# Router columns in the latent product, interleaved first-stage work, expert results added by scatter, and output products placed in the attention drain

## The reference, cut to what matters

```python
xn = layernorm(x)
# layer 0, attention (16 heads, latent): q_latent 192 wide, kv_latent 64 wide, k_rope 64 wide
lat = xn @ [q_a_w, kv_a_w].T ; q_latent, kv_latent = layernorm with weight and bias
scores = (q_nope.k_nope + q_rope.k_rope) * scale ; attn = softmax(scores) @ v ; out @ o_w.T
# layer 0, feed-forward: 32 experts, 4 a token, at most 128 tokens an expert
x2 = w_norm * xn * rsqrt(mean(xn*xn) + 1e-6)
probs = softmax(x2 @ w_router) ; w_topk, sel = top_k(probs, 4)
y[e] = (silu(buf[e] @ w_gate[e]) * (buf[e] @ w_up[e])) @ w_down[e]
out[token] += w_topk * y[e][place]              # tokens past the 128th of an expert are dropped
shared = sigmoid(x2 @ w_shared_gate) * ((silu(x2 @ sw_gate) * (x2 @ sw_up)) @ sw_down)   # 704 wide
x = x + attention + (xn + out + shared)
# layer 1: block-sparse attention and a low-rank expert feed-forward (not touched)
```

## Time and profile before

| what | us |
|---|---|
| runs of the kernel before | 750.59, 755.54, 756.66 (median 755.54) |
| the profiled execution's own time | 748.44 |
| its span, first to last instruction | 746.6 |

### The profile page before, as it was taken

One profiled execution on the slowest core, in us unless ns is written; L12 is line 12 of the kernel. 1 busy time (PEld: TensorE's weight loads), 2 busy tenths in 40 slices (PEclk: granted clock), 3 DMA queues, 4 the chain that ended last, 5 costly groups with the idle time before them and its releaser, 6 DMA issues.

```text
span 746.6 us, 11749 instructions
## 1 busy us (share of the span) xinstructions
PE 710.5 (95%) x3912; PEld 536.0 (72%) x3912; DVE 470.8 (63%) x1336; ACT 357.9 (48%) x928; POOL 262.6 (35%) x252
## 2 busy tenths in 40 slices
PE   4998989899999999998999989999899999999998
PEld 3787868789888898887776656666566648666557
DVE  5798786777887778876885876777633502144311
ACT  2732047688878888788212577898421100011000
POOL 0486125565655655551004248990000250000000
PEclk9999999999999999999999988999999999999999
DMA  8801124534535344343700002000300000000000
GB/s 327 310 1 40 53 81 112 161 112 165 175 99 182 99 162 130 112 146 113 316 1 0 1 1 100 2 2 6 110 0 1 0 1 21 8 0 1 0 1 28
DMA packets 26923, 59.40 MB, mean 80 GB/s; under 512 B 3226, under 2 KB 12956, under 8 KB 26480
## 3 DMA queue, kind: packets, MB, share of 16 engines
q1 hardware_dynamic: 23792, 50.45, 20.1%
q0 software_dynamic: 3072, 8.20, 3.4%
HBM read 48.35 MB, written 10.49 MB: 79 GB/s over the span
## 4 chain that ended last, share of the span: by engine, by line
PE 53%; DVE 10%; ACT 5%; issue 3%; POOL 0%; DMA 0%; DVEq 0%; ACTq 0%; POOLq 0%
PE bank L1975 10%; PE bank L2021 7%; PE bank L1983 7%; PE bank L2033 4%; PE bank L1763 3%; PE bank L1698 3%; PE bank L1867 3%; PE bank L1929 3%; PE bank L1913 2%; PE bank L1783 2%; PE bank L1754 2%; PE bank L1705 2%; PE bank L1774 2%; PE bank L1940 2%; DVE sb L1410 2%
## 5 line engine op out<-in xcount | busy, mean ns | idle before, releaser
L1045 ACT ACTIVATE sb<-bank 128x512 f32<-128x512 f32 x28 | 16.7, 597 | 148.2 <-PE bank L1975 148.2
L909 ACT ACTIVATE sb<-bank,sb 128x256 f32<-128x256 f32 x128 | 59.5, 470 | 40.2 <-DVE sb L1324 38.0
L1763 PE MATMUL bank<-sb 128*128 128x256 f32 x256 | 65.7, 379 | 0.0
L1560 DVE TENSOR_TENSOR sb<-sb,bank 128x512 f32<-128x512 f32 x28 | 19.3, 688 | 73.6 <-ACT sb L1045 73.6
L1324 DVE TENSOR_REDUCE sb<-bank 128x2 f32<-128x512 f32 x64 | 44.1, 689 | 26.0 <-PE bank L1763 24.8
L1009 ACT ACTIVATE sb<-sb 128x128 f32<-128x128 f32 (+1 forms) x128 | 50.6, 444 | 15.7 <-DVE sb L1510 15.1
L916 ACT ACTIVATE sb<-sb 128x256 f32<-128x256 f32 x128 | 57.5, 503 | 0.0
L1975 PE MATMUL bank<-rounded,b_hi 128*128 128x512 f32 x112 | 55.1, 492 | 0.0
L1983 PE MATMUL bank<-sb 128*128 128x512 f32 x112 | 52.8, 594 | 1.2 <-issue 0.7
L735 POOL DMA_INDIRECT sb<-rows_x,sb x32 | 33.0, 1032 | 48.3 <-PE bank L1698 27.2
L1698 PE MATMUL bank<-sb 128*128 128x128 f32 (+1 forms) x384 | 48.8, 277 | 0.8 <-DVE sb L1260 0.8
(11 more groups left out here) (260 smaller groups left out, 1622.9 us busy)
## 6 DMA issues: line engine op xcount, KB each, us to landing
sb<-in_w_gate_up SPq DMA_DIRECT2D x32, 368.0 KB
sb<-in_w_down SPq DMA_DIRECT2D x32, 256.0 KB
sb<-in_w_pair SPq DMA_DIRECT2D x8, 704.0 KB
expert_out<-sb SPq DMA_DIRECT2D x1, 4096.0 KB, 22.2
sb<-expert_out SPq DMA_DIRECT2D x8, 512.0 KB, 7.6
sb<-in_w SPq DMA_DIRECT2D x1, 1792.0 KB, 13.0
sb<-in_b SPq DMA_DIRECT2D x1, 1792.0 KB, 7.6
sb<-in_sw_up SPq DMA_DIRECT2D x1, 1536.0 KB, 8.5
```

What stands on the lines that cost most here:

```text
L909: act.activation(probs[:, u % 4, q, :], bank[3 + u % 2][:, q * S:(q + 1) * S], ACT.Exp, scale=-1.0, bias=row_min[:, u % 4, q:q + 1], accum ...
L1763: mm = pe.matmul(bank[3 + u % 2][:, q * S:(q + 1) * S], qb[i][:, h, b * S + q * P:b * S + (q + 1) * P], keys[:, h, b * S:(b + 1) * S], sta ...
```

## The change

1. The router's 32 columns, the shared gate's one and a column with `w_norm` join `w_lat` (418 columns, 417 of them multiplied). POOL scales the 33 by `w_norm` in place once `w_lat` has landed; PE waits for that before the first latent tile. The router's product (L1620), `w_route` and `x2T` go. DVE scales the 33 columns of all tiles by `rrms` and takes maxima and differences in three operations.
2. The transposes of x2 stand after latent tiles 4 to 7, ACT evicts only the high part, DVE takes the low part from PSUM (`x2_low`), four pieces, the last behind the router's differences. Shared unit 1 waits for all four ahead of its first matmul.
3. The last column tile of the shared part holds 64 gate and 64 up columns, so units 10 and 11 have 6 matmuls instead of 12.
4. The eviction of the transposed latents: three copies go to ACT (`latents_copied`), the two differences stay on DVE. Tiles 2, 3 are turned after unit 11. The addition of xn goes from POOL to ACT: acc = acc * (1 + rstd) - mean * rstd. The router's exponentials come after the first two shared units on ACT.
5. `merge_qk`, `merge_vo` and the four projections of pair 0 stand between the down tiles 4 to 7, in banks of their own. The pair loop waits for six tiles; the eighth is waited for ahead of the first expert. DVE's work on pair 0 stands between the sums in the same way.
6. The zeros go. `rows_x2` rows hold 256 values and 32 probabilities, written by two DMAs; a gather brings both. DVE scales an expert's result by its probability during the eviction. `acc` is written to `expert_sums` after the eighth shared sum, and every store is an indirect DMA that adds to it, issued when the store before it has landed. After the last one SP loads the eight sums into `acc`. The weighted additions L1410 go.
7. CLOSE is experts 26 to 31.
8. Output products of tiles 0 to 3 are issued in the drain, one after each of the first four values, in banks 0, 1, 3, 4. Layer 1's first product waits for four sums instead of eight.

```diff
-CLOSE = (0, 1, 2, 26, 27, 28, 29, 30, 31)
+CLOSE = range(E0 - 6, E0)
+OUT_BANK = (0, 1, 3, 4, 0, 1, 0, 1)
+OUT_AFTER = (0, 0, 0, 0, 1, 2, 5, 6)
-FIRST_TURNS = {2 * NF - 3: (0, 1), 2 * NF - 2: (2, 3)}
+FIRST_TURNS = {2 * NF - 3: (0, 1), 2 * NF - 1: (2, 3)}
+DOWN_BANK, DOWN_AFTER = (0, 1, 2, 3, 0, 3, 1, 2), (0, 0, 0, 0, 1, 4, 2, 3)
...
 # SP
-            sp.wait_ge(zero_set, 1)
-            sp.dma_start(res.rearrange("(r p) d -> p r d", p=P), along(zeros, (1, NT * TOPK0))).then_inc(rows_out_done, 16)
             sp.wait_ge(x2_done, NT)
-            sp.dma_start(rows_x2.rearrange("(t p) d -> p t d", p=P), x2).then_inc(rows_out_done, 16)
+            sp.dma_start(rows_t[:, :, 0:D], x2).then_inc(rows_out_done, 16)
+            sp.wait_ge(rt_step, 5)
+            sp.dma_start(rows_t[:, :, D:D + E0], prob).then_inc(rows_out_done, 16)
...
             sp.wait_ge(rt_dest, 1)
+            sp.wait_ge(rows_out_done, 32)
             for i in range(2):
                 pair_weights(i, i)
+            sp.wait_ge(sh_add, NT)
+            sp.dma_start(sums_t, acc).then_inc(rows_out_done, 16)
...
 # POOL
+            pool.wait_ge(lat_in, 16)
+            pool.tensor_tensor(w_lat[:, :, LATW:LATX], w_lat[:, :, LATW:LATX],
+                               w_lat[:, :, LATX:LATX + 1].broadcast_to([P, KD, E0 + 1]), ALU.mult).then_inc(route_scaled, 1)
...
             def store(e, s):
                 pool.wait_ge(ex_y, e + 1)
+                if e:
+                    pool.wait_ge(y_stored[(e - 1) % SETS], 16 * ((e - 1) // SETS) + 16)
+                else:
+                    pool.wait_ge(rows_out_done, 48)
+                pool.indirect_dma_start(sums[:, :], bass.IndirectOffsetOnAxis(ap=source[:, e:e + 1], axis=0), ye[:, s, :], None,
+                                        bounds_check=TOK - 1, oob_is_err=False, compute_op=ALU.add).then_inc(y_stored[s], 16)
...
 # ACT
+            for u in range(2):
+                shared_hidden(u)
+            act.wait_ge(rt_sub, 3)
+            act.activation(expo, logit, ACT.Exp).then_inc(rt_exp, 1)
+            act.activation(gate_e, scored[:, :, E0], ACT.Exp, scale=-1.0).then_inc(rt_exp, 1)
+            for u in range(2, 2 * NF):
+                shared_hidden(u)
+                for i in FIRST_TURNS.get(u, ()):
+                    latents_copied(i)
+                if 0 <= u - 3 < NT:
...
+                    act.activation(acc[:, i, :], acc[:, i, :], ACT.Identity, scale=grown[:, i:i + 1], bias=shift[:, i:i + 1])\
+                        .then_inc(acc_done, 1)
...
 # DVE
             for i in range(NT):
                 dve.wait_ge(lat_out, i + 1)
...
+                if i:
+                    latent_mean(i - 1)
+                if i > HALF:
+                    x2_low(i - 1)
+            latent_mean(NT - 1)
...
+            dve.tensor_tensor(scored, lat[:, :, LATW:LATX], along(rrms, (2, E0 + 1)), ALU.mult).then_inc(rt_sub, 1)
+            dve.wait_ge(rt_sub, 1)
+            dve.tensor_reduce(route_max, scored[:, :, 0:E0], AX.X, ALU.max).then_inc(rt_sub, 1)
+            dve.wait_ge(rt_sub, 2)
+            dve.tensor_tensor(logit, scored[:, :, 0:E0], along(route_max, (2, E0)), ALU.subtract).then_inc(rt_sub, 1)
+            x2_low(NT - 1)
...
             for i in range(NT):
                 dve.wait_ge(gathered[i], 16)
-                for k in range(TOPK0):
-                    j = i * TOPK0 + k
-                    if k:
-                        dve.wait_ge(combined, j)
-                    dve.scalar_tensor_tensor(acc[:, i, :], picked[:, TILE_AT[i] * TOPK0 + k, :], weight4[:, j:j + 1], acc[:, i, :],
-                                             ALU.mult, ALU.add).then_inc(combined, 1)
                 dve.wait_ge(op_mm, i + 1)
...
 # PE: latents, then the down stage, then the drain
+                if i >= HALF:
+                    turn(i, x2, x2_done)
...
+                if i == HALF:
+                    pe.wait_ge(latT_out, 2 * NT)
+                    merge_qk(0, 0, 0, bank[4])
+                    merge_vo(0, 0, bank[5])
+                if i == HALF + 1:
+                    pe.wait_ge(rt_dest, 1)
+                    pe.wait_ge(at_eff, 1)
+                    project(0, 0, 0, bank[6])
+                    pe.wait_ge(at_eff, 2)
+                    project(0, 1, 0, bank[5])
...
+            pe.wait_ge(sh_add, NT - 2)
...
                 values(g - VALUE_LAG, (g - VALUE_LAG) % UNITS)
+                if g - G < HALF:
+                    attention_out(g - G)
...
-            pe.wait_ge(op_add, NT)
+            pe.wait_ge(op_add, HALF)
```

More of the change, by code:

```diff
@@ L206, in lay_out @@
     kva = f["L0_attn_kv_a_w"]
[L207 to L208 removed]
+    w_lat = np.concatenate([f["L0_attn_q_a_w"], kva[:KVL], kva[KVL:][ROPE_ORDER], swap(kva[KVL:])[ROPE_ORDER]]).T
+    out["w_lat"] = tiles(np.concatenate([w_lat, f["L0_ffn_w_router"], f["L0_ffn_w_shared_gate"],
+                                         f["L0_ffn_w_norm"].reshape(D, 1)], 1))
     wq = f["L0_attn_q_b_w"].reshape(PAIRS, 2, DN, QL).transpose(0, 2, 1, 3)
@@ L379, in program @@
         r2 = strip(region2)
-        lat = r2.take(NT, LATW)
-        w_lat = r2.take(KD, LATW)
-        w_route = r2.take(KD, P)
+        lat = r2.take(NT, LATX)
+        ids = r2.take_b(2, NT * TOPK0, E0)
+        w_lat = Strip(region2, NT * LATX, KD * (LATX + 1)).take(KD, LATX + 1)
         sw_up = r2.take(KD, 2 * NF * P)
@@ L388, in program @@
         onehot = r2.take(NT, TOPK0, E0)
-        place4, over = r2.take(NT * TOPK0), r2.take(NT * TOPK0)
-        slot_id, slot_empty, slot_q, slot_r, token_f, dest_f = (r2.take(E0) for _ in range(6))
+        place4 = r2.take(NT * TOPK0)
+        slot_id, slot_empty, token_f = (r2.take(E0) for _ in range(3))
         hot = Strip(region1, 2 * NT * D, NT * D).take_b(NT * TOPK0, CAP)
-        ids = Strip(region2, NT * LATW, KD * (LATW + P)).take_b(2, NT * TOPK0, E0)
         su_hi = su_hi[:, :].rearrange("p (k n) -> p k n", k=KD)
@@ L851, in turned_copy, with x2_high @@
                     .then_inc(turned_out, 1)
+            def x2_high(g):
+                act.wait_ge(turned, g + 1)
+                act.activation(r(x2T_hi[:, :, (g % 4) * 2 * P:(g % 4 + 1) * 2 * P]),
+                               bank[turn_bank(g)][:, :].rearrange("p (k n) -> p k n", k=KD), ACT.Copy).then_inc(turned_out, 1)
             for g in range(2):
@@ L856, in _ @@
                 act.wait_ge(lat_mm, i + 1)
-                act.activation(lat[:, i, :], bank[4 + i % 2][:, 0:LATW], ACT.Copy).then_inc(lat_out, 1)
+                act.activation(lat[:, i, :], bank[4 + i % 2][:, 0:LATX], ACT.Copy).then_inc(lat_out, 1)
                 if i == 0:
@@ L1214, in _ @@
             dve.wait_ge(rt_step, n)
-            dve.tensor_reduce(place4, flat, AX.X, ALU.add).then_inc(rt_step, 1)
-            dve.wait_ge(rt_step, n + 1)
-            dve.tensor_scalar(over, place4, CAP - 0.5, None, ALU.is_gt).then_inc(rt_step, 1)
-            dve.wait_ge(rt_step, n + 2)
-            dve.scalar_tensor_tensor(weight4.rearrange("p (t k) -> p t k", k=TOPK0),
-                                     over.rearrange("p (t k) -> p t k", k=TOPK0), 0.5, top[:, :, 0:TOPK0],
-                                     ALU.is_lt, ALU.mult).then_inc(rt_dest, 1)
+            dve.tensor_reduce(place4, flat, AX.X, ALU.add).then_inc(rt_dest, 1)
+            for i in range(2, HALF):
+                latents_low(i)
             dve.wait_ge(rt_dest, 1)
@@ L1626, in shared_up @@
                 at_least(pe, sh_act, 2 * u - 2)
-                for j in range(2):
+                if u == 0:
+                    pe.wait_ge(turned_out, 6)
+                if u == 1:
+                    pe.wait_ge(x2_lo, 4)
+                for j in range(2 if f < NF - 1 else 1):
                     tile, cols = slice((j * NF + f) * P, (j * NF + f + 1) * P), slice(c * CH, (c + 1) * CH)
@@ L1828, in _, with attention_out @@
             G = PAIRS * UNITS
+            def attention_out(i):
+                pe.wait_ge(at_ctx, G - UNITS + 2 * (i // QT) + 2)
+                if i == 1:
+                    pe.wait_ge(ex_y, E0)
+                if i in (2, 3):
+                    pe.wait_ge(at_exp, 2 * (G - 3 + i))
+                at_least(pe, op_add, OUT_AFTER[i])
+                for p in range(PAIRS):
+                    mm = pe.matmul(bank[OUT_BANK[i]][:, 0:D], ctxT[:, p, i * P:(i + 1) * P], w_vo[:, p, :],
+                                   start=(p == 0), stop=(p == PAIRS - 1))
+                mm.then_inc(op_mm, 1)
             for g in range(G, G + VALUE_LAG):
```

339 lines of the change are left out of this document (156 added, 183 removed).

## The result

The changed kernel took 744.33 us (median of 4 runs, 738.86 to 747.78), the kernel before 755.32 in the same rounds: ratio 0.9866, 95% interval 0.9829 to 0.9904. Two more measurements on other chips gave 0.9817 (0.9751 to 0.9883) and 0.9870 (0.9831 to 0.9909). The forecast was 739.4 in 730 to 748, faster. So it is faster, by 1.3%, clear of the noise; the median gained 11.0 us where 16.1 were forecast. The profiled execution took 738.86 us; before it was 748.44.

What follows compares the result with a forecast made beforehand. PE was taken to bound the loop, with time to win before it, in PE's waits within it and in the drain. Gains 8.7 + 3.4 + 4.0 = 16.1 us from 755.54 gave 739.4 us, range 730 to 748.

Steps and rivals of the forecast that it cites:

- first rival: Gaps cost clock: ahead of the loop, clock falls and a DVE-bound down stage leave gain 10, 745.4 us; chance 0.20.
- Step 1: Start up to shared unit 1: router product gone, unit 0 at 27.1, unit 1 earlier by 2.0 us.
- Step 2: Shared units from unit 1 to the down stage: down stage at 62.7, 7.5 us earlier, 5.5 added here.
- Table switches: ACT's table loads in the shared units at a higher price: PE waits 2.7 us at unit 4, 742.1 us; chance 0.04.
- Step 3: Down stage and set-up of pair 0: PE's 30.7 us only reordered, loop starts at 93.4, 1.2 us won.
- Step 4: Pair loop: waits for gathered rows and pair 0's queries go, 3.4 us won; adding stores' 3 us landing hidden.
- The experts' phase: Loop: each of 32 gates waits 0.3 us on DVE, 9.6 lost, gain 6.5, 749.0 us; chance 0.08.
- Step 5: Drain and output product: output products cover the drain's idle time, 35.7 us instead of 39.7, gain 4.0.
- Gaps cost clock: Waits ahead of the down stage: two clock falls at 2 us each, plus 2 us in that stage; chance 0.20.
- Scatters bind the loop: Loop, POOL's wait ahead of each store: at a landing of 7.5 us 26 lost, 765.4 us; chance 0.03.

## Why the prediction was right, and where its terms were off

The direction and the range held, and most mechanisms did their work; the gain was smaller than forecast: 11.0 us by the medians, below the 14 to 18 that had the largest chance. That 744.33 lies in the range is due to its width of 18 us. It lies nearer to the first rival's 745.4, but that is no support for its causes: the profiled execution shows none of its two falls of the clock ahead of the loop, and its 2 us in the down stage were to come from DVE. Two of the signs named for being wrong came, a loop of over 247 us in the first trace (247.9) and POOL waiting for its own stores, ahead of half of them. The profiled execution gained 9.6 us and not 16.1: the shared units gave 1.6 less, the down stage 1.9 less, the loop 5.2 less, the drain 1.2 more, layer 1 the clock's 1.1 more.

- **Step 1.** Unit 0 at 27.1 was right to 0.02 us. "Three router operations of 264 columns (0.5 each)" failed: two took 0.43 and 0.42, the third 2.01. The duration came from a row where POOL was quiet. With POOL's subtraction moved away the same instruction took 0.42; with the low part ahead of it, another one fell beside POOL's and took 2.08. The Trainium skill, "SBUF — State Buffer", section "Who interferes with whom", says that DVE and GpSimd share one pair of ports as an exclusive lock, that a `tensor_tensor` with both inputs in SBUF and a `tensor_scalar` in a two-port mode contend for it, and that a reduction never does on trn2. The traces agree for the first and the last, 2.01 us and 0.42 for the reduction; the `tensor_scalar` took 2.08, as the rule has it if it ran in such a mode, which no trace shows.
- **Step 2.** Forecast 62.7 for the down stage, measured 64.34. Unit 1's start carries 1.3 of the 1.6. A wait of 0.62 for ACT at unit 5, units of 2.80 instead of 2.76 us and slower starts behind the waits carry 1.5: from unit 1 to the end of unit 9 it took 26.27 us, forecast 24.75. Against them stand 1.2 us, for the forecast wait for DVE's chain was not there: the chain ended at 59.96, 0.9 earlier than forecast, and PE came 2.7 later. The order of the half units and turns worked as written, and no clock dropped there. ACT's copies and additions stayed hidden.
- **Table switches.** The rival didn't come: loads of 1.28 us with the next activation right behind. ACT was through with unit 2 at 40.97 and PE began unit 4 at 41.05; the wait of 0.62 comes a unit later, where ACT itself had stood 2.60 us for POOL's product.
- **Step 3.** "The rest is PE's own work, 30.7. All of it is kept" failed. The stage took 32.65, 0.7 more than before, though its waits were gone as forecast. The diff's cut of the sixth contraction step to 64 rows, costed at nothing, is 2.7 us. With all rows it is 29.9, so the reordering by itself won 2.0 and not 1.2.
- **Step 4.** "Adding reads the row first; I take 3 us, hidden", and that it costs nothing up to 5, failed. The 3 us were counted from the end of the issue; from there it was 3.9 - 1.6 = 2.3, inside the bound. But I had compared it with the distance between experts, and POOL's work isn't evenly spaced: behind a turning of three instructions (4.0 us) it is late and issues one store as soon as the one before has landed. The issue, taken at 1.0, was 1.6. The store that doesn't add shows the price, 3.4 us in one pair of traces, and with it the loop is the 243 that was forecast. That fit is in part luck: the 2.9 and 0.5 us counted there went, but the waits for DVE's copies of turned rows rose from 0.8 to 2.7, and 1.0 of another wait, ahead of the merged weights, went uncounted. The 2.9 us of gather wait didn't go, it became 2.7 to 8.8.
- **The experts' phase.** Its rival priced the new phase at 9.6 us of waits on DVE. They were 2.6 (before: 0.8); and the phase is a gain, as the kernel with the first experts close again shows, for a reason that stood in none of my cases: it keeps the adding stores away from every other one of POOL's turnings. That cause is read from the traces; no run separates it.
- **Step 5.** Forecast 4.0, measured 5.2, and 5.9 when undone. Its terms, read off the timeline: eight tiles 27.3 (27.6 forecast; 13.98/4 is 3.50, the 3.45 comes from the starts in the earlier trace rows, 358.24 to 372.05), drain work 4.3 (4.9), three turns 1.3 (1.3), the wait ahead of layer 1's product none (0.3), the new wait for the first sum 1.5 (1.6). So the drain work was taken 0.6 too long. The clock was counted, since the sum took the drain work at full clock; how much of the gain is clock only the kernel with the part undone shows, some 3.2 of its 5.9.
- **Gaps cost clock.** Unit 1's wait of 2.42 us was in nine traces. In six of them the granted clock fell to about 0.5 for some 3 us behind it (0.89 or 0.90 in the mean of 15 us from there), in three it stayed at 1.00, the first trace among these; neither of the two without that wait and with POOL in its place had a drop there. So this rival's condition holds in most of the traces, at about 0.6 us (the down stage then starts 37.7 to 37.9 us after unit 0 instead of 37.3), since PE would else have waited for ACT. Its price of 2 us for each fall was set too high here.
- **Scatters bind the loop.** They didn't: a store took 3.9 us to its landing, the issue included, and the loop 247.9 us.

What makes the gather waits differ between traces of one kernel stays open; the stores' longest landings in the seven traces of this loop are 4.9 to 6.8 us, but no run varied the other transfers. The adding store without its wait for the one before wasn't tried, since two stores may add to the same row.

## What to carry to other kernels

Where transfers must follow one another, don't hold their landing against the mean distance between them: look at where their engine comes late and issues several in a row, and at what stands behind each on that engine. Cost an instruction of DVE that works in SBUF alone, however small, by what POOL does at that moment, and look for the reverse too. And work that is laid between the steps of a drain is worth its idle time plus the clock that the idle time would have cost.

## What the runs showed of the hardware that I had not expected

- A weight load of 64 rows among matmuls over 128 rows isn't hidden: the loader stands 0.33 us ahead of it and 0.33 behind it, 0.34 us a tile in all, though half of the rows are saved. Zeros in 128 rows are cheaper.
- Two DVE instructions of 16 and 256 elements, operands and result in SBUF, that start beside a POOL instruction end only behind it: 2.08 and 2.01 us for 0.17 and 0.42. Not all are held: a reduction kept its 0.42 there, and the subtraction that reads one operand from PSUM took 0.68 at 31.81 beside POOL's product, for 0.66 elsewhere. It holds the other way round: five products on POOL of 1.3 us each stretch to 13.80 us beside DVE's unbroken chain, the first alone to 6.67, from the timeline of POOL after:

```profile
36.81 13.80 POOL L715 TENSOR_TENSOR sb<-sb 128x512 f32<-128x512 f32 x5 [3.77 <-ACT sb L894]
```

- An indirect store that adds costs POOL 1.60 us where a plain one costs 1.03, and lands 3.9 instead of 2.5 us after the start of its issue (medians of 32).
